# Mamba stack: softplus as one ScalarE function in place, with a table load of its own, and VectorE left with the product with x

## The reference, cut to what matters

```python
def mamba_block(x, ip_w, cw, cb, xp_w, dtp_w, dtp_b, A_log, Dp, op_w):
    xz = jnp.einsum('bsd,ed->bse', x, ip_w)
    xi, z = jnp.split(xz, 2, axis=-1)
    ...
    xi = jax.nn.silu(conv.transpose(0, 2, 1))
    xdbl = jnp.einsum('bse,fe->bsf', xi, xp_w)
    dt, Bm, Cm = jnp.split(xdbl, [DR_, DR_ + DS_], axis=-1)
    dt = jax.nn.softplus(jnp.einsum('bsr,er->bse', dt, dtp_w) + dtp_b)
    A = -jnp.exp(A_log)
    dA = jnp.exp(dt[..., None] * A)
    dBu = dt[..., None] * Bm[:, :, None, :] * xi[..., None]
    ...  # h = dA * h + dBu along time; y = sum over the 16 states of h * C
    y = ys.transpose(1, 0, 2) + xi * Dp
    y = y * jax.nn.silu(z)
    return jnp.einsum('bse,de->bsd', y, op_w)
```

## Time and profile before

| | |
|---|---|
| median of 3 runs | 5324.02 us (5321.16 to 5324.08) |
| the profiled execution, its own time | 5326.33 us |
| its span in the trace | 5323.6 us |
| mean granted clock of TensorE | 0.956 |
| Mamba stack in the trace | about 0 to 2445 us |
| transformer layers in the trace | about 2445 to 5324 us |

### The profile page before, as it was taken

How to read it: one execution, slowest core, us unless ns; L and a number is a source line. 1 busy time by engine, 2 the same in 40 slices (tenths; PEclk the granted TensorE clock), 3 DMA queues, 4 the chain that set the end, 5 groups by cost and what they waited for, 6 DMA issues and landing times.

```text
span 5323.6 us, 53508 instructions
## 1 busy us (share of the span) xinstructions
PE 4809.0 (90%) x18808; PEld 2634.2 (49%) x18808; DVE 3922.3 (74%) x3821; ACT 2369.1 (45%) x4094; POOL 2613.6 (49%) x1337
## 2 busy tenths in 40 slices
PE   7888898888888889867999789999999999999999
PEld 4455555555555455533555444555544445554444
DVE  4999999999999999985877634666655256665641
ACT  5555655555556555533444333333332233333321
POOL 2555555555555555655888114666600056665000
PEclk8899999999999999988999999999999999999999
DMA  2343444444444443440000010000001000001000
GB/s 106 140 146 137 146 148 146 144 144 146 147 139 143 145 149 133 149 139 24 1 1 13 16 40 1 1 1 1 25 24 40 0 1 1 1 1 48 1 0 16
DMA packets 112901, 372.93 MB, mean 70 GB/s; under 512 B 30080, under 2 KB 34944, under 8 KB 109696
## 3 DMA queue, kind: packets, MB, share of 16 engines
q1 hardware_dynamic: 112640, 369.52, 19.9%
HBM read 366.20 MB, written 3.28 MB: 69 GB/s over the span
## 4 chain that ended last, share of the span: by engine, by line
PE 45%; DVE 6%; ACT 2%; issue 1%; POOL 1%; DVEq 0%; ACTq 0%; POOLq 0%
PE PS L1186 6%; PE PS L1196 6%; PE PS L1211 6%; PE PS L1165 5%; PE PS L1372 5%; PE PS L1383 3%; PE PS L1174 3%; PE PS L1222 2%; PE PS L1332 2%; PE PS L1296 1%; DVE PA L1729 1%; DVE CST L1727 1%; PE PS L1305 1%; PE PS L1152 1%; PE PS L1284 1%
## 5 line engine op out<-in xcount | busy, mean ns | idle before, releaser
L645 POOL TENSOR_TENSOR UH<-UH,BC 128x1152 f32<-128x1152 f32 x512 | 1345.2, 2627 | 1068.3 <-DVE U L714 1068.3
L1131 POOL TENSOR_SCALAR PA<-PA,INV 128x512 f32<-128x512 f32 x768 | 1190.6, 1569 | 548.9 <-DVE INV L1645 548.9
L392 PE MATMUL Y<-UH,ident_sb 128*128 128x512 f32 (+1 forms) x3072 | 1177.1, 528 | 242.7 <-POOL UH L645 135.7
L722 DVE TENSOR_TENSOR_SCAN UH<-DA,U 128x1152 f32<-128x1152 f32 x512 | 1307.1, 2553 | 21.8 <-ACT DA L583 4.4
L392 PEld LDWEIGHTS Y<-UH,ident_sb 128*128 128x128 f32 x3072 | 590.3, 203 | 869.4 <-issue 575.4
L1457 ACT ACTIVATE PA<-PS,NMX 128x512 f32<-128x512 f32 x768 | 519.4, 684 | 718.7 <-DVE NMX L1639 564.4
L583 ACT ACTIVATE DA<-DT,NEGA 128x575 f32<-128x575 f32 x1024 | 718.6, 763 | 107.4 <-DVE UH L722 76.1
L714 DVE TENSOR_TENSOR U<-DTX,BC 128x1152 f32<-128x1152 f32 x512 | 699.2, 1366 | 63.0 <-DMA BC<-bc_rows 10.3
L1654 DVE COPY VP<-PS 128x512 f32<-128x512 f32 x768 | 494.6, 685 | 254.2 <-PE PS L1196 233.1
L1639 DVE TENSOR_REDUCE NMX<-PS 128x2 f32<-128x1024 f32 x384 | 452.3, 1218 | 59.1 <-PE PS L1186 59.1
L1196 PEld LDWEIGHTS PS<-ident_sb,PA 128*128 128x128 f32 x3072 | 350.8, 142 | 241.0 <-issue 195.4
(11 more groups left out here) (162 smaller groups left out, 5309.4 us busy)
## 6 DMA issues: line engine op xcount, KB each, us to landing
BC<-bc_rows SPq DMA_DIRECT2D x512, 576.0 KB, 3.7
ARENA<-mamba_a SPq DMA_DIRECT2D x16, 1421.0 KB, 7.3
ARENA<-pair_w SPq DMA_DIRECT2D x4, 3072.0 KB, 10.6
WB<-mamba_b SPq DMA_DIRECT2D x16, 514.0 KB, 5.0
VP<-ff_w SPq DMA_DIRECT2D x2, 3072.0 KB
WO<-out_w SPq DMA_DIRECT2D x4, 1024.0 KB
stream<-x_t SPq DMA_DIRECT2D x2, 1024.0 KB, 10.1
ARENA<-pair_w SPq DMA_DIRECT2D x4, 512.0 KB, 5.0
```

The source lines that it names most:

```text
L392: mm = pe.matmul(Y[:, a:b], IDENT[:, :], UH[:, SLOT[j], a:b], start=(s == 0), stop=(s == DS - 1), skip_group_check=True)
L645: pool.tensor_tensor(h, h, BC[:, j % NBB, 1, :].unsqueeze(1).broadcast_to([P, HK, T]), ALU.mult).then_inc(s_hc, 1)
L722: dve.tensor_tensor_scan(UH[:, SLOT[j], :], DA[:, j % NDA, :], U[:, 0:HC], 0.0, ALU.mult, ALU.add).then_inc(s_scan, 1)
L1131: pool.tensor_scalar(PR[:, n % 3, j, :], PR[:, n % 3, j, :], INV[:, n % 4, j:j + 1], None, ALU.mult).then_inc(s_ps, 1)
```

## The change

ScalarE reads each dt product once, as identity with bias into DT. In a scan window, after the fourth product (slot 27), it loads the table set "softplus", applies Softplus in place to the two halves of DT (1152 columns each), and loads the set of exp and ln again. In `body(-1)` the set is loaded after the second product, each half is done as soon as its two chunks are there, and the old set is loaded after the fourth. VectorE keeps one instruction for each half, DTX = DT * x (`times_x`), after slots 30 and 31 (for unit 0: ahead of the first window, and after its slot 2). The decays now wait for ScalarE's own softplus (`s_sp`) in place of VectorE's product (`s_dt`, `s_dt2`). The zeros of XPAD are written once, by GpSimd. The buffer LG goes; what it held before the first unit lies in DTX.

```diff
-SOFTPLUS = {27: (0, False), 28: (0, True), 30: (KD, False), 31: (KD, True)}
+DTX_AT = {30: 0, 31: KD}
...
                                 pe.wait_ge(s_xi, START + nxt * KI + i + 1)
                             if i == 0:
-                                pe.wait_ge(s_pad, START + nxt + 1)
+                                pe.wait_ge(s_pad, START + 1)
...
                         if kind == "dt":
                             bias = WA[:, A_DTB + i:A_DTB + i + 1]
-                            act.activation(half(DT[:, bass.ds(off + i * T, T)]), pair(), ACT.Relu, bias=bias)
-                            own(act.activation(E[:, i, :].rearrange("p (a n) -> p a n", a=2), pair(), ACT.Abs, bias=bias))
+                            own(act.activation(half(DT[:, bass.ds(off + i * T, T)]), pair(), ACT.Identity, bias=bias))
                             act.sem_inc(s_free, 1)
-                            if i % 2:
-                                two = slice(i - 1, i + 1)
-                                own(act.activation(E[:, two, :], E[:, two, :], ACT.Exp, scale=-1.0))
-                                act.activation(LG[:, two, :], E[:, two, :], ACT.Ln, bias=SHRC[:, 0:1], scale=SHRINK)
-                                sq = DTX[:, bass.ds(off + (i - 1) * T, KD * T)].rearrange("p (c t) -> p c t", c=KD)
-                                own(act.activation(sq, E[:, two, :], ACT.Relu, bias=EDGC[:, 0:1], scale=-1.0))
-                                act.activation(sq, sq, ACT.Square, bias=EDGC[:, 1:2], scale=-HALF_ROOT).then_inc(s_sp, 1)
+                            if i == (KI - 1 if scan else KD - 1):
+                                act.preload_act_table_set("softplus")
+                            if i == KI - 1 or not scan and i % KD == KD - 1:
+                                for h in range(2) if scan else (i // KD,):
+                                    dt = DT[:, bass.ds(off + h * HC, HC)]
+                                    act.activation(dt, dt, ACT.Softplus).then_inc(s_sp, 1)
+                            if i == KI - 1:
+                                act.preload_act_table_set("natural_log_exp_and_others")
...
                     def decay(j):
                         h, s = j // DS, j % DS
                         if j == DS:
-                            act.wait_ge(s_dt2, START + n + 1)
+                            act.wait_ge(s_sp, START + 2 * n + 2)
...
                     if scan:
-                        act.wait_ge(s_dt, START + n + 1)
+                        act.wait_ge(s_sp, START + 2 * n + 1)
                         act.wait_ge(s_nega, START + n + 1)
...
-                    def pad():
-                        dve.memset(XPAD[:, :, 0:PAD], 0.0).then_inc(s_pad, 1)
-
-                    def softplus(of, k, part_two):
-                        if not part_two:
-                            dve.wait_ge(s_sp, START + of * (KI // KD) + k // KD + 1)
+                    def times_x(of, k):
+                        dve.wait_ge(s_sp, START + of * (KI // KD) + k // KD + 1)
                         o = of % 2 * (KI * T) + k * T
-                        dt = DT[:, bass.ds(o, KD * T)].rearrange("p (c t) -> p c t", c=KD)
-
-                        e, ln = E[:, k:k + KD, :], LG[:, k:k + KD, :]
-                        if not part_two:
-                            own(dve.scalar_tensor_tensor(out=dt, in0=ln, scalar=0.0, in1=dt, op0=ALU.max, op1=ALU.add))
-                            own(dve.scalar_tensor_tensor(out=dt, in0=e, scalar=EDGE, in1=dt, op0=ALU.min, op1=ALU.add))
-                        else:
-                            own(dve.tensor_tensor(DT[:, bass.ds(o, KD * T)], DT[:, bass.ds(o, KD * T)],
-                                                  DTX[:, bass.ds(o, KD * T)], ALU.subtract))
-                            own(dve.tensor_tensor(DTX[:, bass.ds(o, KD * T)], DT[:, bass.ds(o, KD * T)],
-                                                  XS[:, bass.ds(o, KD * T)], ALU.mult))
-                            dve.sem_inc(s_dt2 if k else s_dt, 1)
+                        dve.tensor_tensor(DTX[:, bass.ds(o, KD * T)], DT[:, bass.ds(o, KD * T)], XS[:, bass.ds(o, KD * T)],
+                                          ALU.mult).then_inc(s_dt2 if k else s_dt, 1)
...
-                        if n == 0 and j in (1, 2):
-                            softplus(0, KD, j == 2)
+                        if n == 0 and j == 2:
+                            times_x(0, KD)
...
-                        if prep and j in SOFTPLUS:
-                            softplus(nxt, *SOFTPLUS[j])
+                        if prep and j in DTX_AT:
+                            times_x(nxt, DTX_AT[j])
```

More of the change, by code:

```diff
@@ L303, in _ @@
                 pe.wait_ge(s_pact, START + 2)
-                mid = LG[:, 0:2, 0:256]
+                mid = DTX[:, 0:512].rearrange("p (k n) -> p k n", k=2)
                 for m in range(KD):
@@ L465, in _ @@
                     act.wait_ge(s_pmm, START + m + 1)
-                    act.activation(LG[:, m, 0:256], Y[:, 512 * m:512 * m + 256], ACT.Silu).then_inc(s_pact, 1)
+                    act.activation(DTX[:, 256 * m:256 * m + 256], Y[:, 512 * m:512 * m + 256], ACT.Silu).then_inc(s_pact, 1)
                 act.wait_ge(s_wa, 16)
@@ L486, in body @@
                     hb = (nxt % NB) * T
-                    k0 = 10
+                    k0 = 6
                     step = [0]
@@ L623, in body @@
                     assert not prep or step[0] == k0, step
-                act.wait_ge(s_zero, START + 5)
+                act.wait_ge(s_zero, START + 2)
                 windows(body)
@@ L631, in _ @@
                 pool.memset(EPSC[:, :], EPS).then_inc(s_zero, 1)
-                pool.memset(SHRC[:, :], SHRINK).then_inc(s_zero, 1)
-                pool.memset(EDGC[:, 0:1], EDGE).then_inc(s_zero, 1)
-                pool.memset(EDGC[:, 1:2], EDGE * HALF_ROOT).then_inc(s_zero, 1)
+                pool.memset(XPAD[:, :, 0:PAD], 0.0).then_inc(s_pad, 1)
                 pool.memset(DA[:, :, :], 0.0).then_inc(s_zero, 1)
@@ L650, in _ @@
             def _(dve):
-                step = [0]
                 def final_scale(b):
@@ L668, in body @@
                     uses, base = window_uses(scan, prep, end), before(n, N_PREP, N_END)
-                    def own(ins):
-                        step[0] += 1
-                        ins.then_inc(s_dv, 1)
-                        dve.wait_ge(s_dv, START + step[0])
                     def norm():
@@ L732, in body @@
                         norm()
-                        pad()
-                        softplus(0, 0, False)
-                        softplus(0, 0, True)
+                        times_x(0, 0)
                         return
```

8 lines of the change are left out of this document (removed).

## The result

The changed kernel takes 5179.43 us (median of 4 runs, 5174.22 to 5184.5) against 5324.01 us: the ratio is 0.973 with a 95% interval of 0.9713 to 0.9746, so 2.5 to 2.9% faster. The forecast was 5182 us. The profiled execution has a span of 5179.6 us, 144.0 us less.

The account below looks back on a forecast made before the run. VectorE was taken to bound the Mamba windows. Fifteen windows gave 132.8 us, window 0 another 3.4 and the start 6.0, in sum 142.2 us, so the median of 5324.02 becomes 5182 us, range 5168 to 5210.

Parts of the forecast that it names:

- VectorE bounds the windows, and they gain what leaves its list: Mamba windows: VectorE is busy 96% of the time, so whatever it does beside plain slots lengthens the window fully.
- 8.85 us a window: Steady windows: eight softplus instructions costing 11.25 us go, two products with x at 1.20 us each stay.
- 1.20 in place of the gate's 1.05: Slots 30 and 31: time each product with x adds to a plain slot, taken as 1.20 us, bounds 1.05 to 1.35.
- ScalarE keeps 4.2 us in hand at slot 30: Steady windows: decay(30) ends at about 357.1, 4.2 us ahead of its scan, with Softplus taken as 1.17 us.
- At slot 3 the slack falls from 2.7 to 1.0 us: Next window's slot 3: decay(3)'s lead on its scan shrinks by 1.7 us but should hold.
- The rival of a stall at slot 3: Mean of squares always at the lower clock; VectorE waits about 1 us a window, 15 us back, 5197 us; chance 0.17.
- Window 0 and the start: Window 0 gains 3.4 us more after a new wait; ahead of it 6.0 us go, first scan at about 78.7 us.
- 8.85 + 3.4: Window 0: the steady gain of 8.85 us, plus 4.4 us for the second half less about 1.0 us new wait.
- ScalarE's 7.6 us: Ahead of window 0: 12.6 us of ScalarE work goes, about 5.0 us of Softplus and loads comes, 7.6 us less.
- my 1.6 us: Ahead of window 0: taken off ScalarE's gain because the fourth product waits for the PSUM pair, leaving 6.0 us.
- TensorE does not become the bound: Windows: TensorE at 93% should keep up; the rival, late at gates or UH buffers, costs 51 us, 5233 us, chance 0.08.
- The transformer layers within 5 us: Transformer stage: time left unchanged, with 5 us either way for where TensorE's clock changes fall.

Follow-up runs that it names:

- the two runs with stalls ahead of it: The changed kernel with two and with four more pairs of table loads behind each scan window's softplus: 5230.5 us and 5285.06 us.

## Why the prediction was right, by its steps

- *VectorE bounds the windows, and they gain what leaves its list.* Right: with six instructions put back, 8.57 of the 9.12 us a window came back, and with ScalarE's old chain the windows were as short as with the new one.
- *8.85 us a window.* Measured 9.12. From the scan of slot 27 to that of the next slot 0 it is 22.70 us, averaged over windows 1 to 14, against 31.56 before: 8.86 us, as forecast. The product costs 1.22 us at slot 30 and 1.19 at slot 31 in the window shown, against 1.20. Most of the remaining 0.27 lies at the gate of slot 17, where VectorE waits 0.2 us a window less for TensorE, a wait that I had left as it was; the rest is 0.06 us over the other slots. My reason for 1.20 in place of the gate's 1.05 was only half of it: the product takes 1.46 to 1.50 us because GpSimd's instruction still runs when it starts. In the two runs with stalls ahead of it, where GpSimd had finished, it takes 1.33 us, and slot 31 then lasts 5.11 us, as a slot with a gate does.
- *ScalarE keeps 4.2 us in hand at slot 30.* Right, 4.5. Softplus took 1.155 us where I took 1.17, and the table loads 1.28.
- *At slot 3 the slack falls from 2.7 to 1.0 us.* Wrong in size: in this window it is 3.8 us (`decay(3)` ends at about 634.0, the scan starts at 637.76), and between 2.1 and 3.8 in the others. Two things were off. The window I read had one of the smallest slacks before; they were 2.7 to 3.8 us. And I had left TensorE's adding up and its mean of squares at the lower clock. Before, some of this work ran at the lower clock in all 14 windows; with the change only in windows 1 and 9, and these two are the ones with 2.1 us. In the others TensorE stayed at the full clock (TensorE in order of time, below), which gave ScalarE back more than the shorter slots took. Why the clock stayed up is open: the idle time ahead is shorter (2.30 us, where it was 4.56), but in the same window a product took 3.84 us, at the lower clock, behind only 2.19 us of idle time. The rival of a stall at slot 3 asked for the lower clock throughout; it never came, so the runs do not say what it would have cost.

```profile
610.11 3.84 PE L340 MATMUL PAIR<-HN,ARENA 128*128 128x288 f32 x8 [2.19 <-ACTq L518]
...
622.07 2.21 PE L384 MATMUL Y<-UH,ident_sb 128*128 128x512 f32 x6 [2.30 <-POOL UH L635]
624.11 2.11 PE L340 MATMUL PAIR<-HN,ONES 128*128 128x288 f32 x8
```

- *Window 0 and the start.* 78.78 us for the first scan (78.7 forecast), 0.68 us of new wait at slot 3 (1.0 forecast), 13.27 us for window 0 where my steps have 8.85 + 3.4 = 12.3. That the first scan fits to 0.1 us is luck: in the eleven traces whose preparation of unit 0 is the changed kernel's it starts at 76.4 to 79.0 us. What was lost again of ScalarE's 7.6 us, my 1.6 us, was not measured by itself.
- *TensorE does not become the bound.* Right for the windows as they are. TensorE is busy for 1715 of 1900 us, 90%, where I had 93%, and its granted clock there rose from 0.93 to 0.96. But it is nearer than it looks: with ScalarE 0.7 us beyond its cover, TensorE made a wait of 2.5 us.
- *The transformer layers within 5 us.* 3.3 us longer, less than two traces of one kernel lie apart (8.6 us), and it goes with the time at the lower clock (116.2 us, where it was 109.5).

## What to carry to other kernels

Count what an edit takes off the list of the engine that bounds the stage, with its waits for its own results (here 0.12 us a time). Take a slack from several periods, not one: at slot 3 the window I read had 2.7 us, others 3.8. Work out how far ahead each covered chain ends at the first consumer, and also at the next resource that another engine queues for behind it: 5.1 us more of ScalarE against 4.5 us of cover cost 0.7 us directly and 2.5 us through a PSUM buffer freed late. Spare time on a second engine is no gain if its memory accesses meet those of the bound one.

## What the runs showed of the hardware that I had not expected

- GpSimd and a VectorE instruction with two SBUF operands do not run beside each other: the later one waits for the earlier (3.60 us for a `drive` of 1.37, 3.81 us for the GpSimd product). Beside the scan, with one operand in PSUM, VectorE kept its 2.55 us and GpSimd its 2.62.
- Table loads can stand back to back at 1.28 us each (1.29 from start to start), nine in a row with four extra pairs, with no further cost that the decays or the scans show: the stall of 5.89 us at slot 30 is near 8 x 1.29 - 4.5 = 5.8.
- A shorter list on VectorE left TensorE more often at the full clock. Its mean granted clock over windows 1 to 14 is 0.93 before, 0.94 with VectorE's old load and ScalarE's new chain, and 0.96 with VectorE's new list, whichever chain ScalarE runs. The adding up at slot 0 took 2.21 us after 2.30 us of idle time, where it took 4.21 us after 4.56 us. The idle time just ahead does not settle it alone: 2.19 us of it were followed by a product at the lower clock (3.84 us in place of 2.11) in the same window.
- The transformer layers, the same code in all 13 traces, take 2871 to 2883 us, and on the whole longer with more time at the lower clock there (94 to 122 us). So a difference of under 10 us between two whole times is not yet an effect; it has to be found in the stage that was changed.
- A VectorE instruction with a wait for its own end costs 0.12 us more than one without (10.61 against 9.88 us for six of them).
